# A selective-scan block in float32: twelve of sixteen states summed by accumulating DMAs, products of four channel blocks in one GpSimd instruction

## The reference, cut to what matters

```python
def step(h, inp):
    xt, dtt, bt, ct = inp
    dA = jnp.exp(A[None] * dtt[..., None])
    dB = dtt[..., None] * bt[:, None, :]
    h = dA * h + dB * xt[..., None]
    y = jnp.sum(h * ct[:, None, :], axis=-1)      # over the 16 states
    return (h, y)
...
y = _selective_scan(x_ssm, dt, A, Bm, Cm)
y = y + D[None, None, :] * x_ssm
y = y * z                                         # z = silu(...)
y = y @ w_out.T + b_out
```

## Time and profile before

| what | value |
|---|---|
| median of 3 runs | 4590.73 us (4590.7 to 4592.05) |
| span of the profiled execution, first to last instruction | 4588.9 us |
| PE / DVE / ACT / POOL busy, share of the span | 95% / 80% / 83% / 91% |
| granted TensorE clock, mean | 0.991 |
| mean DMA rate | 56 GB/s |

### The profile page before, as it was taken

How to read it: one execution, slowest core, us unless ns; L and a number is a source line. 1 busy time by engine, 2 the same in 40 slices (tenths; PEclk the granted TensorE clock), 3 DMA queues, 4 the chain that set the end, 5 groups by cost and what they waited for, 6 DMA issues and landing times. The chain is left out here.

```text
span 4588.9 us, 71982 instructions
## 1 busy us (share of the span) xinstructions
PE 4344.2 (95%) x22528; PEld 2805.6 (61%) x22528; DVE 3679.8 (80%) x5132; ACT 3817.6 (83%) x6371; POOL 4161.1 (91%) x3343
## 2 busy tenths in 40 slices
PE   7999999999999999999999999999999999999997
PEld 3666666666666666666666666666666666666664
DVE  3778888888887888888888888888878888888885
ACT  3788888888888888888888888888888888888885
POOL 3899999999999999999999999999999999999995
PEclk8999999999999999999999999999999999999999
DMA  3111111111111111111121111111111111111111
GB/s 129 45 43 58 58 58 45 56 51 57 60 58 48 49 59 59 58 46 54 51 62 59 59 44 56 51 57 60 54 45 54 60 61 58 47 53 51 58 49 39
DMA packets 140915, 254.79 MB, mean 56 GB/s; under 512 B 18597, under 2 KB 18597, under 8 KB 140538
## 3 DMA queue, kind: packets, MB, share of 16 engines
q1 hardware_dynamic: 140538, 250.19, 17.2%
HBM read 215.50 MB, written 34.63 MB: 55 GB/s over the span
## 5 line engine op out<-in xcount | busy, mean ns | idle before, releaser
L364 POOL TENSOR_TENSOR work<-work,c_bc 128x512 f32<-128x512 f32 x2048 | 2590.8, 1280 | 266.6 <-DVE work L1127 180.9
L1127 DVE TENSOR_TENSOR_SCAN work<-work,state,b_ps 128x512 f32<-128x512 f32 x1792 | 2250.5, 1273 | 351.9 <-PE b_ps L453 343.2
L839 ACT ACTIVATE work<-u_td,b_td 128x512 f32<-128x512 f32 x2048 | 1455.4, 711 | 147.5 <-PE b_ps L453 142.2
L829 ACT ACTIVATE work<-dt_t,neg_a 128x512 f32<-128x512 f32 x2048 | 1454.1, 710 | 12.5 <-DVE work L1127 12.1
L453 PE MATMUL b_ps<-ident,work 128*128 128x128 f32 x8192 | 1246.2, 275 | 67.2 <-DVE work L1127 57.0
L453 PEld LDWEIGHTS b_ps<-ident,work 128*128 128x128 f32 x8192 | 966.7, 142 | 344.5 <-issue 173.4
L530 PEld LDWEIGHTS y_ps<-ident,work 128*128 128x128 f32 x6144 | 758.4, 142 | 635.7 <-issue 586.5
L530 PE MATMUL y_ps<-ident,work 128*128 128x128 f32 x6144 | 916.2, 274 | 4.7 <-POOL work L375 3.5
L375 POOL TENSOR_TENSOR work<-work 128x512 f32<-128x512 f32 x512 | 653.4, 1276 | 40.2
L679 PE MATMUL dense<-h_t,w_in_t 128*128 128x512 f32 x1024 | 514.4, 599 | 9.2 <-DVE u_td L1210 8.9
L587 PE MATMUL dense<-w_out_t,proj 128*128 128x512 f32 x1024 | 508.6, 594 | 0.0
(11 more groups left out here) (115 smaller groups left out, 4523.0 us busy)
## 6 DMA issues: line engine op xcount, KB each, us to landing
c_bc<-c_d SPq DMA_DIRECT2D x512, 256.0 KB, 3.2
xn<-in_x SPq DMA_DIRECT2D x128, 256.0 KB, 5.1
x<-in_x SPq DMA_DIRECT2D x128, 256.0 KB, 4.4
out_dram<-x SPq DMA_DIRECT2D x128, 256.0 KB, 4.2
work<-in_wmod SPq DMA_DIRECT2D x2, 1024.0 KB, 6.3
w_in_t<-in_w_in_t SPq DMA_DIRECT2D x2, 1024.0 KB, 9.9
gain_shift<-par_d SPq DMA_DIRECT2D x8, 256.0 KB, 4.5
w_dt_t<-in_w_dt_t SPq DMA_DIRECT2D x1, 1024.0 KB, 11.3
```

Source lines behind the costliest of these rows:

```text
L364: gp.tensor_tensor(pr[:, (s * U + i) % PR_RING, :], hs[:, (s * U + i) % HS_RING, :], c_bc[:, (s * N + n) % C_RING, :], ALU.mult).then_inc( ...
L829: A(decay[:, (s * U + i) % DEC_RING, :], dt_t[:, s % 2, j, :], ACT.Exp, scale=neg_a[:, j, n:n + 1]).then_inc(S["dec_done"], 1)
L839: A(v[:, n % V_RING, tb, :], u_td[:, tb, :], ACT.Copy, scale=b_td[:, s % 2, tb, n:n + 1]).then_inc(S["v_done"], 1)
L1127: V.tensor_tensor_scan(hs[:, (s * U + i) % HS_RING, :], decay[:, (s * U + i) % DEC_RING, :], b_ps[:, i % 2, :], state[:, i:i + 1] if s % N ...
```

## The change

GpSimd's product is one instruction for a state's four channel blocks (128x2048) for states 0 to 13; states 14 and 15 stay unit by unit. The products of states 2 to 13 are written over the scanned states, and a DMA of 1 MB issued by GpSimd adds each to one of two accumulators in SBUF (even states to one, odd to the other, whose first terms are the products of states 0 and 1). The skip term is added by one more such DMA. So there are four sets (0: even states and skip, 1: odd states, 2: state 14, 3: state 15), and PE transposes these four into y_ps: sets 0 and 2 in units 60 to 63, sets 1 and 3 in units 0 to 2 of the next step.

```diff
-    V_RING, DEC_RING, HS_RING, PR_RING, C_RING = 2, 6, 6, 9, 3
-    HELD = (0, 6, 8, 13)
-    SKIP_AT = (8, 9, 10, 11)
-    ORDER = """g.0 g.1 g.2 g.3 g.4 g.5 g.6 yz.0 g.7
+    V_RING, RING, ACC_RING, C_RING = 2, 4 * KD, 3, 3
+    WIDE = N - 2
+    CHAIN = WIDE // 2 - 1
+    SETS = 4
+    ORDER = """g.0 g.1 g.2 g.3 g.4 g.5 g.6 g.7 yz.0
...
+    def set_freed(k, which):
+        at_set = k * SETS + which - ACC_RING
+        return at_set // SETS, (0, 2, 1, 3)[at_set % SETS] * KD + KD
...
+            def wide_product(s, n):
+                at_slot = n * KD % RING
+                states = ring[:, at_slot:at_slot + KD, :]
+                wait_for_c(s, n)
+                gp.wait_ge(S["scan_done"], at("scan_done", s, n * KD + KD))
+                if n < 2:
+                    freed = set_freed(s, n)
+                    gp.wait_ge(S["y_added"], at("y_added", *freed))
+                    out = acc[:, set_slot(s, n), :, :]
+                else:
+                    gp.wait_ge(S["state_done"], at("state_done", s, n + 1))
+                    out = states
+                gp.tensor_tensor(out, states, c_of(s, n).rearrange("p (a t) -> p a t", a=1).to_broadcast([P, KD, T]),
+                                 ALU.mult).then_inc(S["prod_done"], 1)
...
+            def add_to_chain(s, n):
+                at_slot = n * KD % RING
+                gp.wait_ge(S["prod_done"], at("prod_done", s, products(n)))
+                if chain_landed(s, n) > Q:
+                    gp.wait_ge(chain_done[n % 2], chain_landed(s, n) - Q)
+                gp.dma_start(acc[:, set_slot(s, n % 2), :, :].rearrange("p j t -> p (j t)"),
+                             ring[:, at_slot:at_slot + KD, :].rearrange("p j t -> p (j t)"), accum_op=ALU.add
+                             ).then_inc(chain_done[n % 2], Q)
...
                 for i in range(U):
+                    n = i // KD - 1
                     if has_s:
-                        product(s, i)
-                        if summed(i // KD):
-                            add_products(s, i)
+                        if i % KD == 1 and 2 <= n < WIDE:
+                            add_to_chain(s, n)
+                        if i == 10:
+                            add_skip(s)
+                        if i % KD == 0 and 0 <= n < WIDE:
+                            wide_product(s, n)
+                        if i > WIDE * KD:
+                            unit_product(s, i - 1)
                     beside.until(i)
+                if has_s:
+                    unit_product(s, U - 1)
...
+            def add_set(s, which, j):
+                if which == 0:
+                    if j == 0:
+                        pe.wait_ge(S["yzt_done"], at("yzt_done", s - 1, KD))
+                    pe.wait_ge(chain_done[0], chain_landed(s, WIDE - 2))
+                elif which == 1:
+                    pe.wait_ge(chain_done[1], chain_landed(s, WIDE - 1))
+                else:
+                    pe.wait_ge(S["prod_done"], at("prod_done", s, products(WIDE + which - 2, j)))
...
             def turn_y(s, b, c, j):
-                to = inside(s, "g" if j == 0 else "pre.0")
+                to = y_ps[:, j, :]
                 if j == 0:
                     pe.wait_ge(S["y_copied"], at("y_copied", b, TB))
-                    pe.wait_ge(S["zmax_done"], at("zmax_done", b, KD))
-                elif j == 1:
-                    pe.wait_ge(S["gm_done"], at("gm_done", c, 1))
-                else:
-                    pe.wait_ge(S["yzt_done"], at("yzt_done", b, j))
...
-                    if has_b and i < 2:
-                        for r in ((U - 3, U - 2), (U - 1,))[i]:
-                            add_unit(b, r)
-                    if has_s and i >= LAG + 1:
-                        for r in {LAG + 1: (0, 1), LAG + 2: (2,), U - 1: (U - 5, U - 4)}.get(i, (i - LAG,)):
-                            add_unit(s, r)
+                    if has_b and i < 3:
+                        for which, j in (((1, 0), (1, 1), (1, 2), (1, 3)), ((3, 0), (3, 1)), ((3, 2), (3, 3)))[i]:
+                            add_set(b, which, j)
+                    if has_s and i >= U - 4:
+                        for j in ((0, 1), (2, 3))[i % 2]:
+                            add_set(s, 0 if i < U - 2 else 2, j)
...
-                act.wait_ge(S["scan_done"], at("scan_done", s, i + 1 - DEC_RING))
-                A(decay[:, (s * U + i) % DEC_RING, :], dt_t[:, s % 2, j, :], ACT.Exp, scale=neg_a[:, j, n:n + 1]
+                k, r = (s, i - RING) if i >= RING else (s - 1, U + i - RING)
+                if r // KD < 2 or r // KD >= WIDE:
+                    act.wait_ge(S["prod_done"], at("prod_done", k, products(r // KD, j)))
+                    act.wait_ge(S["state_done"], at("state_done", k, r // KD + 1))
+                elif k >= 0:
+                    act.wait_ge(chain_done[r // KD % 2], chain_landed(k, r // KD))
+                A(ring[:, i % RING, :], dt_t[:, s % 2, j, :], ACT.Exp, scale=neg_a[:, j, n:n + 1]
...
-                V.tensor_tensor_scan(hs[:, (s * U + i) % HS_RING, :], decay[:, (s * U + i) % DEC_RING, :],
-                                     b_ps[:, i % 2, :], state[:, i:i + 1] if s % NC else 0.0, ALU.mult, ALU.add
+                V.tensor_tensor_scan(ring[:, i % RING, :], ring[:, i % RING, :], b_ps[:, i % 2, :],
+                                     state[:, i:i + 1] if s % NC else 0.0, ALU.mult, ALU.add
                                      ).then_inc(S["scan_done"], 1)
...
-    nc = bacc.Bacc("TRN2", target_bir_lowering=False, num_devices=1)
+    nc = bacc.Bacc("TRN2", target_bir_lowering=False, num_devices=1, dynamic_dma_scratch_size=2048)
```

More of the change, by code:

```diff
@@ L62, in build_program, with products, skip_landed, chain_landed @@
     TOTAL += 0.8
[L64 to L73, removed]
+    def products(n, j=KD - 1):
+        return n + 1 if n < WIDE else WIDE + (n - WIDE) * KD + j + 1
+    def skip_landed(k):
+        return Q * (k * (CHAIN + 1) + 1)
+    def chain_landed(k, n):
+        return Q * (k * (CHAIN + 1) + 1 + n // 2 if n % 2 == 0 else k * CHAIN + n // 2)
+    def set_slot(k, which):
+        return (k * SETS + which) % ACC_RING
+    def set_freed(k, which):
+        at_set = k * SETS + which - ACC_RING
+        return at_set // SETS, (0, 2, 1, 3)[at_set % SETS] * KD + KD
     def slot(*part):
@@ L141, in build_program @@
         c_bc = sb("c_bc", [P, C_RING, T])
[L143 to L150, removed]
+        work = sb("work", [P, V_RING * TB * D + (RING + ACC_RING * KD) * T])
+        at_ring = V_RING * TB * D
+        at_acc = at_ring + RING * T
+        v = work[:, 0:at_ring].rearrange("p (r b d) -> p r b d", r=V_RING, b=TB)
+        ring = work[:, at_ring:at_acc].rearrange("p (r t) -> p r t", r=RING)
+        acc = work[:, at_acc:].rearrange("p (a j t) -> p a j t", a=ACC_RING, j=KD)
         parts = [work[:, n * KD * D:(n + 1) * KD * D].rearrange("p (k n) -> p k n", k=KD) for n in range(2)]
@@ L177, in build_program @@
             "SP": dict(stored_0=Q, stored_1=Q, stored_2=Q, stored_3=Q, c_stored=Q),
[L178 to L179 removed]
+            "Pool": dict(prod_done=products(N - 1), xsh_done=TB, x1_done=TB, dt_done=KD, u_done=KD, sz_done=KD),
+            "PE": dict(b_made=U, y_added=SETS * KD, s_ps=1, g_used=J, yz_ps=KD, out_ps=TB, res_used=TB, pre_ps=TB, xt_ps=KD, xs_ps=KD,
                        cb_ps=1, bt_ps=1, x2_ps=KD, dt_ps=KD, z_ps=KD, ut_ps=TB),
@@ new lines, in add_skip @@
+            def add_skip(s):
+                gp.wait_ge(S["prod_done"], at("prod_done", s, products(0)))
+                gp.wait_ge(S["skip_done"], at("skip_done", s, KD))
+                if s:
+                    gp.wait_ge(chain_done[0], skip_landed(s) - Q)
+                gp.dma_start(acc[:, set_slot(s, 0), :, :].rearrange("p j t -> p (j t)"),
+                             xs_t[:, :, :].rearrange("p j t -> p (j t)"), accum_op=ALU.add
+                             ).then_inc(chain_done[0], Q)
@@ L986, in sigmoids @@
                     yield from sigmoid(s, m, made("z", m, 3) + 1)
-            AHEAD = DEC_RING - 2
+            AHEAD = KD
             V_AHEAD = TB + 2
@@ L1164, in take_y @@
                     dve.wait_ge(S["sz_done"], at("sz_done", b, j + 1))
-                    V.tensor_tensor(yz_t[:, j, :], sz_t[:, j, :], inside(s, "g" if j == 0 else "pre.0")[:, :], ALU.mult
+                    V.tensor_tensor(yz_t[:, j, :], sz_t[:, j, :], y_ps[:, j, :], ALU.mult
                                     ).then_inc(S["yzt_done"], 1)
```

93 lines of the change are left out of this document (34 added, 59 removed).

## The result

| | before | after |
|---|---|---|
| median of the runs | 4590.72 us | 4934.27 us (4929.93 to 4938.51) |
| span of the profiled execution | 4588.9 us | 4928.2 us |
| one mid-run chunk | 139.2 us | 149.3 us |

The ratio is 1.075, with a 95% interval of 1.0735 to 1.0765: 343.6 us slower where the forecast was 93 faster, and 104 us beyond the range's upper end.

What follows compares the result with a forecast made beforehand. PE was taken as the bound, POOL close behind. Greatest engines 133.9 plus waits 0.5 and 1.9 gave 136.3 us a chunk, 2.9 less; over 32 chunks 93 us less, 4498 us. Range 4230 to 4830, the forecast's own 4440 to 4560.

Steps and rivals of the forecast that it cites:

- Prices: On POOL a wide product 4.6 us and an accumulating DMA's issue 1.0; that DMA's landing 8.5 us.
- C: POOL becomes the bound: wide product 5.12 us, issue 1.7; 145.2 us a chunk, 4783 us; chance 0.22.
- D: Accumulating DMAs land late, at 17 us, passing today's pace at 15: 148.8 us a chunk, 4898 us; chance 0.18.
- the list of new waits: Small work queues behind POOL's long instructions; with the lock, 1.9 us a chunk added in window 4.
- i = 24: Unit 24: last addition of `attended` stands behind state 5's wide product; DVE's statistics wait 1.7 us.
- i = 52: Unit 52: last product of `step_size` is late; PE waits where POOL binds, so nothing extra is added.
- the sum: Greatest engine of each window, 133.9, plus 0.5 old and 1.9 new waits: 136.3 us a chunk against 139.2.
- window: One of eight stretches of a mid-run chunk, cut at every eighth scan; each counts its greatest engine.
- Two of its signs: Expected in the profile: PE matmul busy down 450 to 610 us; POOL almost never idle in units 40 to 63.
- rival B: Cheap issues on POOL, 0.3 us each: 130.4 us a chunk, 4310 us, or 4230 with overlap; chance 0.13.
- The bunch: PE's 16 y_ps additions come eight each in windows 8 and 1, 3.5 us each; PE 17.5 and 18.0.
- The lock: Window 4: DVE's L1140 must sit out POOL's wide product, both using SBUF; 2.6 us of wait.

Runs made afterwards that it cites:

- second experiment: Changed kernel with SP issuing each row of C three units later: 4685.27 us, ratio 1.0207 to the kernel before.
- the control: Kernel before the change, with the rows of C issued three units later: 4589.19 us, ratio 1.0000.
- first experiment: Changed kernel with POOL's small work put ahead of the wide product in units divisible by four: 4822.78 us, ratio 1.0508 to the kernel before.
- the version with both orders: Changed kernel with small work ahead of the wide product and C's rows issued three units later: 4500.81 us, ratio 0.9808 to the kernel before.

## Why the prediction was wrong

**Prices: about right.** Wide product 4.56 (4.6 taken), issue 0.90 (1.0), landing 8.1 (8.5), all from the change's own profile. POOL's chunk is 109.7 us busy where 112.4 was worked out, DVE 113.4, ACT 119.3 as before. Rivals C and D, which held the slower cases at 4783 and 4898, were both about these prices, and both are refuted: issues under 1.3 us, and a landing far from the 15 us at which it would have passed the old pace. The time landed near D's number by another cause.

**The step that failed: the list of new waits stops at POOL's own program.** "New waits come from POOL's long instructions, behind which small work queues" is followed by two places in POOL's order, i = 24 and i = 52. `spread_c` is not mentioned: POOL's wait for x, behind SP's queue, stands in the sum at nothing, without a reason, and was 264 us, 8.3 a chunk. The change lengthened what SP waits for, from a state's last 1.28 us product to a product of 4.56 us over the whole state, and behind that wait stand the reloads of x. The second experiment prices this at 249 us in the change, 322 once small work goes first, and the control shows that the place of C's rows was free before. Two waits of the kernel before, of SP's queue and of POOL, show how it looked:

```profile
SPq L298 <- POOL work L364: 3747.9, 478, 13.9
```

```profile
POOL x L384 <- DMA x<-in_x: 12.8, 3, 9.3
```

SP stood most of the span behind POOL's products already, and the reloads behind it still came early enough. What they become when that product is four times as long was not asked.

**The term at nothing: i = 52.** "At i = 52 the last product of `step_size` is late too, but PE, which needs it, waits in a window where POOL binds and is counted." The place and the mechanism were right, the covering was not: PE waited for that product in every chunk, 6.5 us in the mean and 7.0 at most. PE held the transposes and so DVE's scans (DVE stood 5.58 us in window 7), and POOL then stood 2.84 us for scanned states. A sum of the greatest engine per window counts work, and here each of the three waited for the next. The first experiment took 111 us back by moving nothing but the order within a unit, and 184 on top of the second.

**The term for i = 24 was of the right size.** 1.7 us a chunk were taken. DVE waited 8.5 us a chunk for POOL's additions in the change, but over three of them, with x late. With C's rows issued later and the wide product still ahead of the last addition, the same wait was 59.1 us in 33 times, 1.8 a chunk. So what the sum lacked here came from SP's queue as well.

**The sum itself.** Without these two places, the forecast of 4498 us is what the version with both orders measures, 4500.81, and 136.3 us a chunk became 136.9. That is partly luck, since errors of both signs cancel: the windows were forecast at 18.0, 18.2, 15.7, 17.4, 16.0, 16.2, 16.2, 18.1 and came as 18.9, 19.5, 17.1, 15.0, 15.9, 13.8, 17.9, 18.8. Two of its signs failed as well: PE's busy time was to fall by 450 to 610 us and fell by 214, by 335 (to 4009.3) with both orders; and POOL was to be almost without idle time in units 40 to 63, where in window 6 of the change it was busy for 11.4 of 13.7 us. Two readings in it are slips that change no sum: in rival B the 14.8 of window 6 is POOL's (PE's own there is 11.9), and the earlier trace rows have three rows at 1.28, not four.

**The bunch.** PE in windows 1 and 8 was forecast at 18.0 and 17.5 and was busy 18.3 and 18.8: right, and in the change the two windows got slower by 2.3 and 2.6 us.

**The lock.** In the change L1174 (the old L1140) took 0.141 to 0.166 us in all 64 cases: the 2.6 us of the sum were not there. The lock is real, the order just never met it. In window 4 L1174 began at 2241.43 us, and POOL, which waited for the same state's copy, began its wide product at 2241.70. The lock is back in the first experiment (a median of 0.17 us, at most 1.37) and with both orders (0.16, at most 1.97), where the prediction looked for over 2 us in half the cases; DVE's and POOL's timelines in the first:

```profile
2048.81 1.20 DVE L1177 SCALAR_TENSOR_TENSOR norm<-norm 128x4 f32<-128x4 f32 x1
```

```profile
2045.47 4.51 POOL L378 TENSOR_TENSOR work<-work,c_bc 128x2048 f32<-128x2048 f32 x1
```

It began 1.17 us before the wide product's end (2049.98) and lasted 1.20. So the rule of the Trainium skill ("SBUF — State Buffer", section "Who interferes with whom"), that such a DVE instruction and one of GpSimd which reads SBUF exclude each other, agrees with the wide product too. The scans, which have one input in PSUM, kept their 1.27 us beside wide products, as the rule has it.

**The clock.** It was not in the prediction. The granted clock was 1.00 in all eight windows of the earlier trace rows and 0.85, 0.90 and 0.94 in windows 4, 7 and 8 of the change; with both orders mended it is 1.00, 0.92 and 0.98. Behind the 6.99 us of idle time in the rows above it was low, so part of the price of a wait is paid after it: 0.5 us for each of the two sets of transposes and 1.4 for the four matmuls. How much of the 343 us is the clock's was not measured by itself. Estimates from above, as if all of PE's longer work were the clock's and on the path: PE was busy for 4129.9 us in the change, 237 more than 4344.2 less the 451 taken out, of the 343; and 121 more than the 4009.3 of the version with both orders, which runs the same 18432 matmuls, of the 433 between those two.

## What to carry to other kernels

When an instruction gets four times as long, list everything that queues behind it on its own engine, and then every queue that waits for its end, the DMA issuer's too, with what stands behind that wait; a busy engine's sum says nothing of it. Put short work that others wait for ahead of the long instruction, and issue DMAs that wait on it late enough that the wait is already over. Two in-order queues that wait for each other's long work make a loop that no window of busy time shows: look for a time that rose while no engine got busier.

## What the runs showed of the hardware

- An accumulating DMA of 1 MB from SBUF to SBUF landed in 8.1 us, a plain copy of the same size in 5.7, and the queue's share of the engines went from 43.3% to 21.4%: the accumulation costs the engines twice the time. The Trainium skill ("Collectives: The Full Stack", section "The bandwidth ceiling") puts such a factor, there for reductions between the cores of a chip, down to the second source that must be read; the factor of 43.3 to 21.4 agrees, what makes it no run here separates.
- An accumulating DMA's issue takes 0.90 us of GpSimd, a plain copy's of the same size 0.59 (means of 384). The 128x512 instruction right behind an accumulating one has a longer record, 1.58 in place of 1.27 us, and the mean of the unit products is 1.425 us, where the earlier trace rows have 1.280 and the version with plain copies 1.274. But the records overlap: one issue began at 2305.03 us and the three instructions behind it at 2305.64, 2306.87 and 2308.11, still 1.2 us apart. So the longer records are no price beyond the 0.90.
- After 7 us without a matmul, PE ran at the lower of its two clock levels, 1.2 GHz in place of 2.4 (granted clock 0.50), through the next two sets of transposes and most of the four matmuls behind them (0.54 in the mean): 1.12 and 1.06 against 0.60 us, 3.31 against 1.88.
